# A two-layer decoder on one core: where the causal mask is added, where carried waits stand, and another order of the steps

## The reference, cut to what matters

```python
# layer 0: RMS norm, cross-attention to ctx, 16 heads of 64, no mask
q, k, v = normed @ wq, ctx @ wk, ctx @ wv
x = x + softmax(q k^T) v @ wo
# layer 1: 16 heads of 16
h = mha(ln(x), ln(x), ..., causal=True)      # scores = where(tril, scores, -inf)
x = x + h @ m_proj_w + m_proj_b
h = mha(ln(x), ctx, ..., causal=False)
x = x + h @ c_proj_w + c_proj_b
x = x + relu(ln(x) @ f_w1 + f_b1) @ f_w2 + f_b2
```

## Time and profile before

| | |
|---|---|
| median of 3 runs | 5888.48 us (5873.54 to 5890.43) |
| the profiled execution | 5875.75 us |
| its span, first to last instruction | 5874.0 us |
| PE busy | 5309.4 us, 90% |
| ACT busy | 4329.6 us, 74% |
| DVE busy | 2190.4 us, 37% |
| POOL busy | 530.7 us, 9% |
| mean granted TensorE clock | 0.952 |

### The profile page before, as it was taken

The page is one execution under the profiler, slowest core; times in us unless marked ns, Lnnn a source line. Parts: engine busy times, 40 slices in busy tenths (PEclk is TensorE's granted clock), DMA queues, the critical chain, the costliest instruction groups (busy, mean ns, idle before and its releaser), DMA issues. The chain is left out here.

```text
span 5874.0 us, 137598 instructions
## 1 busy us (share of the span) xinstructions
PE 5309.4 (90%) x48328; PEld 4185.2 (71%) x48328; DVE 2190.4 (37%) x5823; ACT 4329.6 (74%) x17665; POOL 530.7 (9%) x845
## 2 busy tenths in 40 slices
PE   6989999999999899999999998999899999999997
PEld 5767777677777677777777777777677777777775
DVE  3334333333333343333333333433333334334332
ACT  3777777787777777777877777778778777777785
POOL 0001001000000010010000000100100001001000
PEclk9999999999999999999999999999999999999998
DMA  2000000000000000000000000000000000000000
GB/s 69 10 12 10 14 11 11 14 8 14 14 8 14 12 10 14 10 12 14 8 14 14 8 14 12 10 14 8 14 14 8 14 12 10 14 12 10 14 8 8
DMA packets 64805, 76.10 MB, mean 13 GB/s; under 512 B 4592, under 2 KB 62768, under 8 KB 63920
## 3 DMA queue, kind: packets, MB, share of 16 engines
q1 hardware_dynamic: 63920, 64.19, 3.5%
HBM read 47.40 MB, written 16.78 MB: 11 GB/s over the span
## 5 line engine op out<-in xcount | busy, mean ns | idle before, releaser
L452 ACT ACTIVATE ps<-ps,negmax 128x77 f32<-128x77 f32 (+2 forms) x6144 | 2070.5, 377 | 255.4 <-DVE negmax L664 255.4
L452 ACT ACTIVATION_READ_ACCUMULATOR ps<-ps,negmax 128x1 f32 x6144 | 1542.6, 255 | 0.0
L664 DVE TENSOR_REDUCE negmax<-ps 128x4 f32<-128x308 f32 (+2 forms) x1792 | 929.5, 563 | 699.5 <-PE ps L891 349.7
L405 POOL TENSOR_TENSOR small<-small 128x1 f32<-128x1 f32 (+1 forms) x448 | 263.5, 588 | 5148.7 <-DVE small L638 2674.8
L659 DVE TENSOR_TENSOR zTl<-ps,zTh 128x256 fp32r<-128x256 f32 x512 | 210.6, 422 | 1241.4 <-ACT zTh L432 1241.4
L838 PE MATMUL ps<-wf,coT 128*128 128x256 f32 x2048 | 475.7, 385 | 10.9 <-issue 7.8
L838 PE MATMUL ps<-wo,coT 128*128 128x256 f32 x2048 | 469.4, 382 | 0.2 <-issue 0.2
L517 ACT ACTIVATE probs<-ps 77x512 f32<-77x512 f32 x512 | 275.5, 588 | 229.2 <-PE ps L943 226.2
L838 PEld LDWEIGHTS ps<-wf,coT 128*128 128x128 f32 x2048 | 379.8, 190 | 90.6 <-issue 43.8
L525 ACT ACTIVATE probs<-ps 128x512 f32<-128x512 f32 x768 | 388.2, 617 | 63.7 <-PE ps L982 63.7
L838 PEld LDWEIGHTS ps<-wo,coT 128*128 128x128 f32 x2048 | 379.2, 190 | 56.9 <-ACT ps L452 10.0
(11 more groups left out here) (181 smaller groups left out, 11816.6 us busy)
## 6 DMA issues: line engine op xcount, KB each, us to landing
xin<-x_dram SPq DMA_DIRECT2D x64, 256.0 KB, 3.4
x<-x_dram SPq DMA_DIRECT2D x64, 256.0 KB, 2.7
out<-xr SPq DMA_DIRECT2D x64, 256.0 KB, 4.0
cin<-ctx_dram SPq DMA_DIRECT2D x64, 77.0 KB
wk<-wk_dram SPq DMA_DIRECT2D x1, 1024.0 KB, 5.3
wo<-wo_dram SPq DMA_DIRECT2D x1, 1024.0 KB, 8.1
wf<-f_dram SPq DMA_DIRECT2D x1, 1024.0 KB, 10.6
probs<-wq_dram SPq DMA_DIRECT2D x1, 1024.0 KB, 9.9
```

The costliest lines, as they stand in the source:

```text
L405: nc.gpsimd.tensor_tensor(rstd[:, stage, ts], veps[:, stage, ts], minus_half[:, ts], ALU.pow).then_inc(rstd_ready[stage], 1)
L452: ins = nc.scalar.activation(scores, scores, ACT.Exp, bias=negmax[w][:, t, h:h + 1], accum_out=sums[w][:, t, h:h + 1])
L664: nc.vector.tensor_reduce(dst, bank(s)[:, 0:heads * width].rearrange("p (h k) -> p h k", h=heads), AX_X, ALU.max, negate=True).then_inc(ma ...
```

## The change

Four things are changed.

1. The mask matmuls L920 and L971 are removed, with the identity in bf16. DVE adds the triangle in place in the bank instead (new function `masks`: one tensor_tensor of 128x256 or 128x512 for each bank, in1 a bf16 triangle in SBUF). In `qsA` and `qsB` the four adds stand ahead of the four maxima, which wait for them through `chain`. In `skA` and `skB` ACT's exponential waits for a new semaphore `masked` instead of `full`. A transposed triangle is made once by POOL.
2. The waits for what an earlier turn made are moved from the end of the turn to the steps that read it, on PE and ACT. `Counts` now knows the turn before, and the banks' semaphores begin at 24.
3. SP issues, in a turn, the loads of `x1`, `xin` and `cin` ahead of the store of `y`; `xin` and `cin` are those of the turn that follows.
4. `LOOP_ORDER_TEXT` is another order.

```diff
-    k1- pv.2.0 pv.2.1 qsB.1- cv- proj.2.1 proj.2.0 stat.3.0 ck- stat.3.1 norm.3.0 ctx+ v1- qsB.0-
-    norm.3.1 turn.3.0 k0.0+ k0.1+ turn.3.1 v0.1+ qsA- ln.1- h.0 h.3 h.2 h.1 v0.0+ qs0.1.2+ qs0.1.3+ mt.1-
...
+    ck- pv.2.0 pv.2.1 cv- ctx+ qsB.0- k0.0+ qsB.1- qsA- proj.2.0 stat.3.0 proj.2.1 stat.3.1 norm.3.0
+    ln.1- k0.1+ v1- q0.3+ v0.1+ q0.1+ v0.0+ norm.3.1 turn.3.0 mt.1- turn.3.1 qs0.1.0+ qs0.0.0+ qs0.1.3+
+    skB- h.0 h.3 h.2 h.1 skA.0- qs0.0.2+ qs0.0.3+ qs0.1.1+ qs0.1.2+ qs0.0.1+ f2.0 ln.0+ pv.1.0- skA.1-
...
+            def masks(u, heads, mask, at, added):
+
+                for s, v, _ in u["bank"]:
+                    dve.wait_ge(full[s], v)
+                    scores = bank(s).rearrange("p (h k) -> p h k", h=heads)[:, :, at:at + P]
+                    nc.vector.tensor_tensor(scores, scores, mask[:].unsqueeze(1).to_broadcast([P, heads, P]),
+                                            ALU.add).then_inc(added, 1)
...
             def maxima(u, j, dst, heads, width):
                 s, v, _ = u["bank"][j]
+                if "chain" in u:
+                    dve.wait_ge(chain, u["chain"][j][1])
...
+                    elif n in ("skA", "skB"):
+                        masks(u, 2 if n == "skA" else 4, causalT, 0, masked)
                     elif n == "qsA":
+                        masks(u, 4, causal, 0, chain)
...
                     elif n in ("skA", "skB"):
                         for r in range(4):
-                            s = landed(u, r)
+                            (s, _, _), (_, _, total) = u["bank"][r], u["masked"][r]
+                            act.wait_ge(masked, total)
...
-                        for s, _, _ in u["bank"]:
-                            heads = 4 if n == "qsA" else 2
-                            diagonal = bank(s).rearrange("p (h k) -> p h k", h=heads)[:, :, 512 // heads - P:]
-                            pe.matmul(diagonal, identb[:], causal[:].unsqueeze(1).to_broadcast([P, heads, P]),
-                                      start=False, stop=True, skip_group_check=True).then_inc(full[s], 1)
...
-                        for r in range(4):
-                            s = take_bank(u, r)
-                            diagonal = bank(s).rearrange("p (h q) -> p h q", q=cols)[:, :, 0:P]
-                            pe.matmul(diagonal, causal[:], identb[:].unsqueeze(1).to_broadcast([P, len(heads), P]),
-                                      start=True, stop=False, skip_group_check=True)
...
-                landed(c, {"bank": []}, *CARRIED)
+                if c.settle:
+                    for step, reader in CARRIED:
+                        if step in c.of:
+                            for s, v, _ in c.of[step]["bank"]:
+                                pe.wait_ge(free[s], v)
```

More of the change, by code:

```diff
@@ L17 @@
 MASKED = -1e30
-RINGS = {"bank": 8, "split": 1, "chain": 1, "max": 1}
+RINGS = {"bank": 8, "split": 1, "chain": 1, "max": 1, "masked": 1}
+FIRST = 24
 USES = {
@@ L30 @@
     "ck": {"bank": 1}, "cv": {"bank": 1}, "q1": {"bank": 1}, "k1": {"bank": 1}, "v1": {"bank": 1},
-    "qsA": {"bank": 4, "max": 4}, "qsB": {"bank": 4, "max": 4}, "qs2": {"bank": 4, "max": 4},
-    "skA": {"bank": 4}, "skB": {"bank": 4}, "sk2": {"bank": 4},
+    "qsA": {"bank": 4, "max": 4, "chain": 4}, "qsB": {"bank": 4, "max": 4, "chain": 4}, "qs2": {"bank": 4, "max": 4},
+    "skA": {"bank": 4, "masked": 4}, "skB": {"bank": 4, "masked": 4}, "sk2": {"bank": 4},
     "pv": {"bank": 1, "split": 1}, "proj": {"bank": 1},
@@ L145, in next, with all, source @@
         return taken
+    def all(self, order):
+        for step in order:
+            self.next(step)
+        return self
+    def source(self, step, reader):
+        if STAGES[step] == STAGES[reader]:
+            return self.of.get(step)
+        return self.past.of.get(step) if self.past else None
 def wait(eng, sem, value):
@@ L172, in decoder @@
              (part(0, 1), 1, (NB - 1, NB - 2, None)), (part(1), 1, (None, NB - 1, None))]
-    before = {r: [0] * n for r, n in RINGS.items()}
+    before = {r: [FIRST if r == "bank" else 0] * n for r, n in RINGS.items()}
     turns = []
@@ L305, in orders @@
         def orders(eng, run):
-            for order, before, uses, count, batch in turns:
+            past = None
+            for k, (order, before, uses, count, batch) in enumerate(turns):
                 if batch is not None:
-                    run(order, Counts(before, None, 0), batch)
+                    past = Counts(before, None, 0, past, turns[min(k + 1, len(turns) - 1)][4] is None)
+                    run(order, past, batch)
                 else:
                     with eng.Fori(0, NB - 2) as i:
-                        run(order, Counts(before, uses, i), (i + 1, i, i + 2))
+                        earlier = {r: [a - b for a, b in zip(before[r], uses[r])] for r in RINGS}
+                        run(order, Counts(before, uses, i, Counts(earlier, uses, i).all(order)), (i + 1, i, i + 2))
+                    last = {r: [a + (count - 1) * b for a, b in zip(before[r], uses[r])] for r in RINGS}
+                    past = Counts(last, None, 0).all(order)
         def probs_slot(step, r):
@@ L545, in run @@
                         ins.then_inc(free[s], 1)
[L548 removed]
+                if c.settle:
+                    for st in CARRIED_SUMS:
+                        if st in c.of:
+                            for s, v, _ in c.of[st]["bank"]:
+                                act.wait_ge(free[s], v)
             act.wait_ge(consts_ready, 1)
@@ L616, in _ @@
                                                  ALU.mult))
+            for bank_free in free:
+                dve.sem_inc(bank_free, FIRST)
             dve.sem_inc(consts_ready, 3)
@@ L709, in run @@
                         m = step[1]
+                        masks(u, 2, causal, P, chain)
                         for r in range(4):
@@ L782, in _ @@
             pe.wait_ge(consts_ready, 1)
+            for bank_full in full:
+                pe.sem_inc(bank_full, FIRST)
             def take_bank(u, j=0):
```

113 lines of the change are left out of this document (64 added, 49 removed).

## The result

| kernel | median of its runs | ratio to before |
|---|---|---|
| before | 5889.45 us (5873.54 to 5894.07, 4 runs) | |
| changed | 5524.84 us (5510.36 to 5533.2, 4 runs) | 0.9383, 95% interval 0.9356 to 0.9409 |

The account below looks back on a forecast made before the run. PE, busy 90% of the span, was taken as the bound. Masks -224, waits -55, loads 0, adds and order +186 sum to -93 us from 5875.75, 5783 us, forecast as 5785 us; range 5660 to 5925 us.

Parts of the forecast that it names:

- The return: PE's idle time before `mt.0` at a turn's start: 3.9 us of it are the loop's return, kept by the change.
- the second rival: Adds hidden by the order, or clock kept at 1.00 by a shorter return: 5640 us; chance 0.17.
- Loads: `x1`, `xin`, `cin` ahead of the store on SP: counted 0, bounds -20 and +10 us, as PE doesn't wait for DVE there.
- Waits: Moved from the turn's end to their readers: 0.9 us a turn, -55 us, bounds 25 to 85 us saved.
- Masks, adds and order: Masks leaving PE save 224 us; DVE's adds and the new order cost 186 us (120 to 265).
- the walk: Steps from `qsB.0` to `qsA` on 8 banks: `qsA` ends at 8.8 us, PE idle 3.7 us of them.
- the bank ring costs a second slow stretch: From `qsB.1` to `qsA` the clock falls too: +167 us, 5950 us if in each turn; chance 0.15.
- My argument against it: Against a clock fall from `qsB.1` to `qsA`: idle pieces of 1.4 us and less; `qsB`'s 0.55 us wait lies at 1.00.
- the order hides the adds: ACT less behind or adds cheaper, so only masks and waits count: 5640 us; chance 0.17.
- The masks' 224 us: Mask matmuls leaving PE: 3.5 us a sequence, times 64, -224 us (220 to 237).
- The sign: The whole change was called faster, with chance 0.75; same 0.11, slower 0.14.

Follow-up runs that it names:

- padded kernel before: Kernel before with 32 tiny matmuls (128 instructions) added ahead of the loop on PE, loop untouched: 5642.45 us, 0.9555.
- pad of 40: Changed kernel with 10 tiny products (40 instructions) added ahead of the loop on PE: 5726.50 us, 0.9703.
- with 200 ahead: Old order, masks on PE, waits at readers, loads ahead of the store (5313.99 us), plus 50 tiny products (200 instructions) ahead of the loop: 5474.37 us, 0.9278.
- changed kernel's pads: Changed kernel with 24, 32, 40, 48 or 64 instructions of tiny products ahead of the loop: 0.9494, 0.9578, 0.9703, 0.9346, 0.9356.

## Why the prediction was wrong

The ladder of ratios gives each part its size, in shares of 5889 us and in this order of steps: the fetch at the return -262 (1 to 0.9555), loads -249 (to 0.9133), waits -77 (to 0.9002), order +79 (0.9136), masks moved to DVE +145 (0.9383). The sum is -364, where the prediction has -93.

- **The return: the step that failed.** "So all data is there by 3031.7, and the other 3.9 us are the loop's return itself, which this change keeps." The time was read rightly, its cause was named without a row. Two other sentences name PE's instruction fetch at the return, but as something fixed, which the change could neither end nor bring back. It was a fetch of nine pieces of program a turn, which stops where the body touches seven (by the edges worked out below), and the change moved the body by that little: it begins 25 instructions earlier and is 43 shorter. The part 3 row of 568 packets was on the page. A shift with no other edit, 128 instructions later, gives the kernel before 262 us.
- **The clock at the return** stayed at 1.00, as the second rival had it. In the padded kernel before the records' sum fell from 485 to 253 us; the fall now comes some 6 us behind the return, in the wait for `zTl`. So of the 262 us some 116, half of the difference, is clock; that is an estimate.
- **Loads, priced at 0 (-20 to +10): -249 us.** "None of PE's longer waits is for `turn.0`" was true only under the cover of the return's idle time. I named no cover for it. With the return gone it is the next stall, and the clock falls on it.
- **Waits, priced at -55: -77 behind the loads, 0 alone.** This term was right in size (25 to 85) and in mechanism: 0.9 us a turn were forecast at `mt.0`, 1.1 are gone there. Without the loads the same time goes to `xin`.
- **Masks, adds and order, priced together at -224 + 186 = -38: +224 us (0.9002 to 0.9383), the other step that failed.** Of these +79 are the order with masks on PE and +145 the masks' move. The sizes of the walk were right: four adds of 128x256 take 1.42 us (0.42 + 3 x 0.34 = 1.44), four of 128x512 2.49 (0.69 + 3 x 0.60 = 2.49), and `qsA` ends 10.1 us after `qsB.0` begins instead of 8.8, the last part at half clock. The rival "the bank ring costs a second slow stretch" happened in every turn, though it is now the only one, since the return has none; its own sum, -224 + 186 + 167 = +129, has the right sign and is 95 short of 224. The page TensorE: Matmul & The Clock Gate of the Trainium skill, "HAM oscillation", tells of a kernel in which waits between bursts of matmuls brought the clock down in every tile. The trace agrees in that it falls in every turn; but here no single wait is long, those labelled between `qsB.0` and `qsA` are 0.15 to 0.50 us. My argument against it (idle time in pieces of 1.4 us and less) does not hold.
- **The order, not priced by itself:** it costs 79 us with masks on PE, but with masks on DVE it takes 0.9859 to 0.9383, 280 us less. It makes the adds bearable rather than hiding them, so the rival "the order hides the adds" is false although its number was the nearest.
- **The masks' 224 us** are a price only as long as nothing waits behind PE: 70 us in the old order, and in the new 0.0184, 108 us, for one pass of the two.

The sign was right by luck: without the return and the loads the terms come to +147 us (-77 + 79 + 145), measured on bodies that stay. Had the body come to lie as with the pad of 40, the same change would have shown 0.9703, some 5715 us, 70 below the forecast and inside the range; how the terms divide there no run tells.

## What to carry to other kernels

Read the instruction queue's row before calling a loop's return a fixed cost: packets in a multiple of the turns (here nine for each) were the program fetched anew, and a few dozen instructions more or less ahead of the loop took 4% off the kernel before, and put 3% on the changed one. Compare two versions of a kernel only when both bodies stay, or the layout is taken for the edit. When a stall goes, whatever lay beside it (here a load behind a store) has to be priced again as if the stall had never been there.

## What the runs showed of the hardware

- TensorE's program of 4815 instructions (changed kernel) to some 5050 (kernel before, padded) came through q8 in 19 packets of some 16 KB where no turn fetched; the one of 5164, with 200 ahead, has 20 beside its 34 times nine. So a packet holds about 250 to 270 instructions. Bodies of 1560 to 1610 instructions stayed or not by their place alone: 1475 to 3085 stays, 1451 to 3054 is fetched in every turn. With edges taken as every 256 instructions, one between 1466 and 1474, all bodies of the study fit: those that stay touch seven pieces, those that are fetched eight. The edges are inferred; no trace shows them, nor why a turn fetches nine packets. How many turns fetch, in one execution of each kernel, rises with how far the eighth piece is entered: if the edge is at 1470, then 4, 12, 20 and 48 instructions past the last edge go with 6, 31, 41 and 61 turns, and 23 with 34 in the kernel with 200 ahead. What decides in a given turn stays open. The Trainium skill says that TensorE holds 128 KiB, 2048 instructions, in blocks of 16 KiB (Runtime: NRT & Kernel Launch, "Instruction fetch mechanics"). The runs agree that a whole body of 1610 can stay, and show that one of 1603 may not.
- A fetching turn is 2.8 us longer where the clock stays up, 4.4 to 4.8 in the changed kernel's pads (88.02 and 83.59 us; 88.70 and 83.89), 3.8 in the kernel before (89.87 and 86.04).
- DVE's add of the bf16 triangle in place in PSUM takes 423 ns for 128x256 and 691 for 128x512 (mean of L706 in the changed kernel), as the fp32 tensor_tensor forms before (692 ns): the mixed case that no run before showed costs the same.
